# First routed block's rows built by 0/1 products, and unread products placed in the last steps of the first self-attentions

## The reference

```
x = x + cross_attention_0(norm(x), context)
x = x + self_attention_0(norm(x))            # "mla"
x = x + block_0(norm(x))                     # self-attention ("ffn"), then a mixture of experts
x = x + cross_attention_1(norm(x), context)
x = x + self_attention_1(norm(x))
x = x + dense_0_1(norm(x))
```

```
m     = layernorm(x) * ln2_g + ln2_b
probs = softmax(m @ Wg)                      # 8 experts
wts, idx = top_k(probs, 2)                   # two experts for each row
ye[e] = gelu(m @ W1[e] + b1[e]) @ W2[e] + b2[e]
x     = x + sum of wts * ye[idx]
```

## Time and profile before

| | |
|---|---|
| median of 3 runs | 1070.48 us (1069.71 to 1071.32) |
| the profiled execution: its own time | 1078.87 us |
| its span in the trace | 1076.4 us |
| PE busy | 95% of the span |
| DVE, ACT, POOL busy | 60%, 44%, 23% |
| mean granted clock of TensorE | 0.968 |
| load of a block's rows (`xg`), issue to landing, median of 15 | 7.9 us |
| the chain that ended last: PE's share | 86% |

### The profile page before, as it was taken

One profiled execution on the slowest core, in us unless ns is written; L12 is line 12 of the kernel. 1 busy time (PEld: TensorE's weight loads), 2 busy tenths in 40 slices (PEclk: granted clock), 3 DMA queues, 4 the chain that ended last, 5 costly groups with the idle time before them and its releaser, 6 DMA issues.

```text
span 1076.4 us, 27540 instructions
## 1 busy us (share of the span) xinstructions
PE 1024.8 (95%) x11721; PEld 884.5 (82%) x11721; DVE 640.7 (60%) x1377; ACT 470.0 (44%) x863; POOL 244.2 (23%) x381
## 2 busy tenths in 40 slices
PE   5999999999999999999489999997999999999998
PEld 5888888888888778887389999996888888887887
DVE  5655545545333546765649999986577663454242
ACT  3333333333333565633146677762534443463231
POOL 2311311211110224343404444422212000011000
PEclk9999999999999999997589999999999998998999
DMA  9400000000000710220136557612111002000000
GB/s 310 129 2 21 21 1 21 2 1 1 2 1 2 285 61 3 85 95 12 51 80 235 196 196 263 238 57 79 42 51 41 3 2 70 3 2 2 0 21 19
DMA packets 55673, 72.79 MB, mean 68 GB/s; under 512 B 8505, under 2 KB 48897, under 8 KB 54913
## 3 DMA queue, kind: packets, MB, share of 16 engines
q1 hardware_dynamic: 54016, 66.85, 18.6%
q0 software_dynamic: 1536, 4.20, 1.2%
HBM read 60.02 MB, written 11.01 MB: 66 GB/s over the span
## 4 chain that ended last, share of the span: by engine, by line
PE 86%; DVE 7%; issue 2%; ACT 2%; POOL 1%; DMA 1%; DVEq 0%; POOLq 0%; ACTq 0%
PE ps L616 8%; PE ps L631 8%; PE ps L2243 7%; PE ps L2259 7%; PE ps L2599 6%; PE ps L1504 4%; PE ps L600 3%; PE ps L1422 3%; PE ps L648 3%; PE ps L1138 3%; PE ps L668 2%; PE ps L1461 2%; PE ps L1521 2%; PE ps L570 2%; PE ps L1063 2%
## 5 line engine op out<-in xcount | busy, mean ns | idle before, releaser
L371 POOL TENSOR_TENSOR rn_tmp<-rn_cur,eps 128x1 f32<-128x1 f32 x48 | 14.1, 293 | 359.2 <-DVE rn_cur L365 359.0
L759 ACT ACTIVATE x0pT<-ps 128x512 f32<-128x512 f32 x64 | 38.3, 598 | 123.6 <-PE ps L631 123.6
L2395 DVE CAST eh_hi<-eh 128x512 fp32r<-128x512 f32 x60 | 67.8, 1130 | 14.2 <-ACT eh L2305 14.2
L2243 PE MATMUL ps<-moe_xT_hi,ew_1hi 128*128 128x256 f32 x240 | 69.9, 291 | 2.3 <-DVE moe_xT_lo L2389 2.3
L2259 PE MATMUL ps<-ew_2hi,eh_hi 128*128 128x256 f32 x240 | 69.4, 289 | 2.4 <-DVE eh_lo L2397 2.4
L2243 PE MATMUL ps<-moe_xT_lo,ew_1hi 128*128 128x256 f32 x240 | 69.0, 288 | 0.0
L2243 PE MATMUL ps<-moe_xT_hi,ew_1lo 128*128 128x256 f32 x240 | 68.9, 287 | 0.0
L2259 PE MATMUL ps<-ew_2hi,eh_lo 128*128 128x256 f32 x240 | 67.0, 279 | 0.0
L2259 PE MATMUL ps<-ew_2lo,eh_hi 128*128 128x256 f32 x240 | 66.8, 279 | 0.0
L2599 PE MATMUL ps<-f,ffw 128*128 128x512 f32 x256 | 61.5, 402 | 0.8 <-issue 0.6
L868 DVE TENSOR_TENSOR x0A_lo<-ps,x0A_hi 128x512 fp32r<-128x512 f32 x64 | 41.1, 685 | 31.8 <-ACT x0A_hi L750 31.7
(11 more groups left out here) (334 smaller groups left out, 2831.9 us busy)
## 6 DMA issues: line engine op xcount, KB each, us to landing
ew<-L_ffn_W_dram SPq DMA_DIRECT2D x30, 1024.0 KB, 7.2
x0cin<-ctx_dram SPq DMA_DIRECT2D x8, 512.0 KB, 4.1
x1cin<-ctx_dram SPq DMA_DIRECT2D x8, 512.0 KB, 4.4
xg<-moe_in SPq DMA_DIRECT2D x15, 256.0 KB, 7.9
moe_out<-moe_y SPq DMA_DIRECT2D x15, 256.0 KB, 7.6
moe_in<-padneg SPq DMA_DIRECT2D x3, 1024.0 KB, 13.1
maskrow<-mask_BxS_ik_dram SPq DMA_DIRECT2D x2, 1024.0 KB, 7.7
x0wk<-L_xattn_Wkv_dram SPq DMA_DIRECT2D x1, 1024.0 KB, 7.2
```

Of the source, the lines that this page charges most:

```text
L759: nc.scalar.activation(g.pT[:, u, :], ps[:, S_BANK[u % 2], :], ACT.Exp, scale=64.0 ** -0.5).then_inc(C0.exp, 1)
L2243: last = nc.tensor.matmul(ps[:, n % 3, j * BT:j * BT + BT], w[b % 2][:, i, f * P:f * P + P], v[b % 2][:, i, :], start=(i == 0 and m == 0), ...
L2395: nc.vector.tensor_copy(eh_hi[n % 3][:, :], eh[n % 3][:, :]).then_inc(MO.hi, 1)
```

## The change

- `find_slots` (DVE, two instructions of 128 x 256) compares a row of the numbers 0 to 255 (`slot_no`, made once by `number_slots` in six small instructions at step 4) with the two slot numbers of each of a tile's rows. The result, `hot[t]`, is 1 where row p of tile t belongs in slot j of block 0, and 0 elsewhere.
- `place` (PE, two float32 products of 128 x 128 on 256 columns) multiplies the tile's normalised rows u by `hot[t]` and accumulates over the 8 tiles in PSUM banks 4 and 5: the rows of block 0, already transposed. ACT reads them there. The load `rows_of(0)` and the transpose `rows_T(0)` of PE are gone; `rows_of(1)` waits in addition for the last `place`.
- `keep_clock` is called in steps 14, 15 and 16 between the halves of the values product (3, 2 and 2 products of 128 x 128 on 256 columns), and once more in step 15 (2 products) ahead of the transpose.
- In step 17 `moe_norm` of the last item stands ahead of `route_slot_top` on DVE; on POOL the scatter of tile 4 stands behind the statistics and the addition of the last item.
- The computation of the owners of blocks 8 to 14 and their biases (`owners`, `owners_biases`) moves behind `rows_T(0)` on DVE, and in part behind the first pieces of the expert stage.

```diff
+            def place(t):
+                pe.wait_ge(MO.hot, t + 1)
+                for k in range(KD):
+                    last = nc.tensor.matmul(ps[:, FIRST_BANK + k, 0:BT], u[:, t, k * P:k * P + P], hot[t][:, :],
+                                            start=(t == 0), stop=(t == T - 1), skip_group_check=True)
+                if t == T - 1:
+                    last.then_inc(MO.xT_ps, 1)
...
+                    if span == 0 and hi - 2 <= n <= hi:
+                        RS.wait_free(pe, n - 1, "T")
+                        keep_clock(RS.bank(n - 1, "T"), 3 if n == hi - 2 else 2)
                     if back:
                         fill_pv(n - 1, 1)
+                final = n - hi if span == 0 else None
                 if routed(span, n - 3):
                     fill_router(n - 3)
+                if final == 1:
+                    place(3)
+                if final == 2:
+                    place(5)
...
+                if final == -1:
+                    RS.wait_free(pe, n - 1, "T")
+                    keep_clock(RS.bank(n - 1, "T"), 2)
+                if final == 0:
+                    place(0)
                 if back:
                     fill_T(n - 1)
...
+                if final == 0:
+                    place(1)
+                    place(2)
+                if final == 1:
+                    place(4)
+            if span == 0:
+                for t in range(6, T):
+                    place(t)
...
+                if final == 1:
+                    moe_norm(n - 2)
                 if routed(span, n - 4) or routed(span, n - 3):
                     route_slot_top(dve, n - 4 if routed(span, n - 4) else None, n - 3 if routed(span, n - 3) else None)
...
+                if final == -2:
+                    find_slots(dve, 0)
+                    find_slots(dve, 1)
                 if back:
                     residual(n - 1)
+                if final == 2:
+                    find_slots(dve, 6)
                 if routed(span, n - 3):
                     route_rank(dve, n - 3)
+                if final == 1:
+                    find_slots(dve, 5)
+                if final == -1:
+                    find_slots(dve, 2)
+                    find_slots(dve, 3)
+                if final == 0:
+                    find_slots(dve, 4)
+                if final == 3:
+                    find_slots(dve, 7)
...
-                if routed(span, n - 4):
+                if routed(span, n - 4) and n != hi:
                     scatter(n - 4)
...
+                if routed(span, n - 4) and n == hi:
+                    scatter(n - 4)
...
+        def find_slots(dve, t):
+            dve.wait_ge(MO.slot_no, 6)
+            dve.wait_ge(MO.route, ROUTE[t, "slotf"])
+            if t > 0:
+                dve.wait_ge(MO.hot, t)
+            nc.vector.tensor_scalar(hot_too[:, :], slot_no[:, :], slotf[:, t, 1:2], None, ALU.is_equal).then_inc(MO.hot_too, 1)
+            dve.wait_ge(MO.hot_too, t + 1)
+            nc.vector.scalar_tensor_tensor(hot[t][:, :], slot_no[:, :], slotf[:, t, 0:1], hot_too[:, :], ALU.is_equal, ALU.add).then_inc(MO.hot, 1)
...
-            rows_T(0)
             hidden(0)
             hidden(1)
...
+                    src = ps[:, XT_BANK, k * BT:k * BT + BT] if b > 0 else ps[:, FIRST_BANK + k, 0:BT]
+                    last = nc.scalar.activation(xT[:, k, :], src, ACT.Identity,
...
             rows_T(0)
+            owners()
             hidden(0)
             hidden(1)
...
+                if n == 1:
+                    owners_biases()
...
-                if b > 1:
-                    sp.wait_ge(MO.xT_ps, b - 1)
+                sp.wait_ge(MO.xT_ps, max(b - 1, 1))
...
-            rows_of(0)
             rows_of(1)
```

More of the change, by code:

```diff
@@ L1967, in dve_self @@
                     norm(n + 3)
-                if routed(span, n - 2):
+                if routed(span, n - 2) and final != 1:
                     moe_norm(n - 2)
+                if final == -2:
+                    find_slots(dve, 0)
+                    find_slots(dve, 1)
                 if back:
                     residual(n - 1)
+                if final == 2:
+                    find_slots(dve, 6)
                 if routed(span, n - 3):
                     route_rank(dve, n - 3)
+                if final == 1:
[7 more added lines that the diff above has]
+                    find_slots(dve, 7)
+                if span == 0 and n == 4:
+                    number_slots(dve)
                 if span == 0 and n in (3, 5, 7, 9):
@@ L2039, in build @@
             spread = sem("mo_spread")
+            slot_no = sem("mo_slot_no")
+            hot = sem("mo_hot")
+            hot_too = sem("mo_hot_too")
             owner = sem("mo_owner")
@@ L2096, in route_rank, with number_slots @@
             nc.vector.tensor_tensor(slot_e[:, :], rank, block_off[:, :], ALU.add).then_inc(SA.by_dve, 1)
+        def number_slots(dve):
+            nc.vector.tensor_copy(slot_no[:, 0:E], cst[:, C_IOTA:C_IOTA + E]).then_inc(MO.slot_no, 1)
+            for i in range(5):
+                w = E << i
+                dve.wait_ge(MO.slot_no, i + 1)
+                nc.vector.tensor_scalar(slot_no[:, w:2 * w], slot_no[:, 0:w], float(w), None, ALU.add).then_inc(MO.slot_no, 1)
+        def find_slots(dve, t):
[6 more added lines that the diff above has]
+            nc.vector.scalar_tensor_tensor(hot[t][:, :], slot_no[:, :], slotf[:, t, 0:1], hot_too[:, :], ALU.is_equal, ALU.add).then_inc(MO.hot, 1)
         def route_slot_top(dve, a, b):
@@ L2164, in build @@
         XT_BANK, O_BANK = 3, (4, 6)
+        FIRST_BANK = 4
         def expert_part(b, i):
```

40 lines of the change are left out of this document (23 added, 17 removed).

## The result

The changed kernel takes **1063.2 us** (median of four executions, 1062.1 to 1063.7), where the kernel before took 1070.9 beside it (1069.7 to 1072.1): a ratio of 0.9932, with a 95% interval of 0.9913 to 0.995. The forecast was 1063.2. Timed again in five rounds, the changed kernel had a median of 1063.4 and the kernel before 1070.0, but the spread was another one: eight of twelve executions within 1062.0 to 1063.5, one of 1069.5 and three of 1073.1 to 1073.6. With these the ratio is 0.9967 (0.9939 to 0.9996). So the size of the median was right, and one execution of four takes 6 to 10 us more. Most of the experiments turned out to be about that.

A forecast was written before the change was run, and what follows sets the result against it. PE was taken to bound the kernel, slowed by half clock from 497 us and waiting on block 0's row round trip. Gains 2.4 - 0.2 + 5.3 = 7.5, less 0.2 for small covers, 7.3: 1070.5 to 1063.2 us, range 1058.5 to 1069.

The forecast's parts named there:

- Up to Y: End of step 13 to end of the last output product: 27.0 us becomes 24.6 at full clock, 2.4 earlier.
- From Y to S: End of the last output product to the last slot numbers: 12.5 us becomes 12.75, 0.2 later.
- From S to H: Last slot numbers to first expert product: 10.55 us becomes 5.2 without the round trip, 5.3 won.
- Behind H: From the first expert product on: nothing gained, since hidden products start at half clock as before; earlier gain carried through whole.
- rival 3: Expert stage: the DRAM round trip moves to block 1, a slow load costing up to 2.8 us: 1066; chance 0.06.
- rival 4: Steps 14 to 16: DVE becomes the bound through five more comparisons, 4 us if most on path: 1067; chance 0.08.
- Rival 1: Steps 14 to 16: clock falls anyway, unread products paid at half clock: 1079; chance 0.08, another 0.08 falling in step 16.
- The rule on shared interfaces: Comparisons on the path: POOL contention could hold each up to 0.55 us, 1.1 together, giving 1064.3; nothing was added.

The follow-up runs named there:

- old order: Changed kernel with VectorE's and GpSimd's old order in the last two steps (norm and last scatter where they stood before): 1064.3 us, ratio 0.9961.
- unread only: Kernel before with the nine unread products alone, block 0's rows still from HBM: 1070.3 us median of twelve, ratio 1.0019.
- hold: Changed kernel with 14 further unread products up to the expert stage: 1063.0 us, ratio 0.9958; timed again 1060.7 us, ratio 0.993.
- one piece: Changed kernel with its seven unread products ahead of both halves of the values product instead of between them: 1062.8 us median of six, ratio 0.9939.
- no unread: Changed kernel without its nine unread products, 0/1 products and new DVE and POOL order kept: 1065.8 us median of nine, ratio 0.9966.
- double: Changed kernel with seven more unread products, six, four and four between the halves instead of three, two and two: 1066.7 us median of twelve.

## Why the prediction was right, point by point

**The view on which it rested** showed an execution that is not the usual one. The prediction saw that its profile stood 8.4 above the median and took the gain to be the same in both. That step was wrong in its parts and right in its sum. In the two later profiles of before A is 24.1 and 24.2 and not 27.0, so against these the held clock gains 0.8 and not 3.6.

**Up to Y** the forecast had 27.0 going to 24.6; the profile of after has 23.4. The terms: the unread products took 4.6 instead of 4.2 (1.50 + 1.06 + 0.95 + 1.06 by starts), the place 0.94 instead of 0.95, the wait in step 15 is 0.73 instead of 1.0 and is for ACT's `sa_mT`, with none for DVE's read of the counts. The rest took 17.1 instead of 18.4: that is no more than the bare sum at full clock, 17.3, although waits of 0.28 and 0.47 are in it; the 1.1 added for small waits was too much.

**From Y to S** 12.75 were forecast, and 12.8 measured (515.53 to 528.35). The forecast had the norm 1.9 earlier; it is 2.4. In the old order it is 1.8 more to S, 0.6 of it by the order and 1.2 because place and router then stood at half clock.

**From S to H** 5.2 were forecast, and 5.2 measured, with the place at half clock as taken (2.09). It is also 5.2 in the old order. This is the safest number of the case: it is the round trip that went, and B is about 5 shorter without it (17.8 to 18.1 against 23.1 to 23.5) whatever the clock did before Y.

**Behind H** nothing was forecast; C is 186.3 in both first profiles. Block 1's rows were no wait (rival 3): their transpose is at 540.67, behind the first 36 hidden products. The comparisons beside the residual did not become the bound (rival 4): PE's waits in steps 14 to 16 are the 0.73 and the 0.47 seen above, and one of 0.28 for DVE's `sa_att`.

**The sum.** Between the second and third profile of before and the two of after it is 0.8 in A, 5.2 in B, 0.1 in C, and 0.4 that step 13 ended earlier: 6.5 of span, where 7.3 were forecast and the medians differ by 7.7 and 6.6. The mis-sized term is the one up to Y, 2.4 forecast and 0.8 measured between these profiles. That the median came out at 1063.2 to a tenth is luck within this.

**Rival 1** got 0.08, with another 0.08 for a later fall. Long executions are real: three of sixteen of after took 1073.1 to 1073.6, one 1069.5, where the rival had 1079. The reason given for it, that three unread products had not saved the clock at 897, was the better one; the reason against it, that the product there stood in one piece, does not hold: the clock also fell at 499 to 500 where the halves were cut apart (old order, the second profile of unread only, the third of hold), and the kernel with both halves in one piece took no longer. With that falls the prediction's reading that narrow products cut up by wide ones keep the clock. That a fall near 500 makes executions long was seen in two kernels of which a long one was profiled. None of the changed kernel itself was. The late falls, which cost 5 to 6 where they were seen, are too short for its 1073 but could make its 1069.5; this is open.

**The rule on shared interfaces.** The prediction weighed up to 0.55 for a comparison beside POOL's addition; its rows give 0.49 (0.66 less 0.17, of two different instructions, and the same instruction took 0.15 in the profile of after with no addition beside it). In step 16 of after the second comparison of a tile ran beside POOL's addition and took 0.89 instead of 0.48:

```profile
511.61 0.71 POOL L2054 TENSOR_TENSOR x_res<-x_res,u 128x256 f32<-128x256 f32 x1
511.71 0.89 DVE L2174 SCALAR_TENSOR_TENSOR hot<-slot_no,slotf,hot_too 128x256 f32<-128x256 f32 x1
```

The Trainium skill, "GPSIMD Engine Reference", section 1 (Specifications), which has POOL contend with DVE instructions of two SBUF inputs, agrees with this row. The two comparisons on the path at 528 took 0.35 and 0.48, with no addition beside them, and nothing was to be added.

## What to carry to other kernels

Take the round trip out of the chain first: rows that go to HBM and back by slot number can be put in place for the first block by 0/1 products. Of the 6.5 us, 5.2 came from there and from the new order of DVE and POOL together (3.3 were left of it in the old order, in a profile where the place and the router of step 17 stood at half clock), and this did not depend on the clock before Y. Unread products to hold the clock are a bet: they cost their full-clock time when they work and twice that when they don't, and alone they gained nothing here; on top of the 0/1 products they took 2.4 to 3.0 us off the median. Before a change of that kind is judged, profile the kernel before several times and count executions, since one profile may show a state that most of them never have, and a median hides the quarter that goes wrong.

## What the runs showed of the hardware that was not expected

- With the same instructions in the same order, the granted clock held in one execution and fell near 500 us in another (A 22.9 and 32.5, and 23.4 and 34.5). From 490 to 500 us TensorE was occupied 9.72 of 10 us in the profiles of after and of hold, where the clock held, and just as long in those of one piece and of hold's third, where it fell at 500, and of no unread, where it fell at 496. The Trainium skill, "TensorE: Matmul & The Clock Gate", section "Part 1: The HAM clock gate", lays the clock to how busy TensorE has been recently; occupied time alone does not tell these apart. What does is open; shifting the stretch in time by itself was not tried.
- The fall is not tied to an undivided piece of narrow products. It came at 499 to 500 us with wide ones between the halves (old order, unread only, hold), and with the wide ones beside the piece instead of inside it the time was the same.
- A fall near 500 us in spite of unread products lasted either 3 to 8 us (one piece, old order, double) or 27 to 51 us (the two long profiles). Without any, the clock came back within 4 to 14 us in three profiles of four. What ends a fall was not tried.
- Late falls, at 894 to 904 and 982 to 993 us, lie in code that all kernels share, were in two of fourteen profiles, and cost 5 to 6 us together (D 346.8 and 346.9 against 340.9 to 341.8 of the same kernels). One near 740 us is in thirteen of the fourteen.
